# Adaptive layer norm, causal attention and a routed feed-forward layer on one core: maxima and masks fused, block masks spread over partitions by DMA

## The reference, cut to what matters

```python
mod = (silu(c) @ wmod)                      # six rows of 128: sa, ca, ga, sb, cb, gb
ga, gb = sign-preserving clamp of ga, gb to magnitude >= 0.25
h = layernorm(x) * (1 + ca) + sa            # x is (1, 2048, 128)
q, k, v = h @ Wq + bq, h @ Wk + bk, h @ Wv + bv
w = softmax(causal(q @ k.T / sqrt(128)))    # 2048 x 2048, causal
x = x + ga * ((w @ v) @ Wo + bo)
h = layernorm(x) * (1 + cb) + sb
prob = softmax(h @ w_router + b_router)     # 16 blocks; the 4 best are kept for each token
mask = top-4 of prob, one entry for each block of 32 hidden channels
y = relu(h @ w1.T + b1) * mask(per block) @ w2.T + b2     # 512 hidden channels
out = x + gb * y
```

## Time and profile before

| | |
|---|---|
| time, median of 3 runs | 129.37 us (129.15 to 129.53) |
| the profiled execution: its own time | 129.4 us |
| its span, first to last instruction | 127.7 us |
| mean granted clock of PE | 0.996 |
| PE busy | 120.7 us (95%) |
| DVE, ACT, POOL busy | 85.1, 75.5, 72.0 us |

### The profile page before, as it was taken

The page is one execution under the profiler, slowest core; times in us unless marked ns, Lnnn a source line. Parts: engine busy times, 40 slices in busy tenths (PEclk is TensorE's granted clock), DMA queues, the critical chain, the costliest instruction groups (busy, mean ns, idle before and its releaser), DMA issues.

```text
span 127.7 us, 2080 instructions
## 1 busy us (share of the span) xinstructions
PE 120.7 (95%) x655; PEld 95.2 (75%) x655; DVE 85.1 (67%) x300; ACT 75.5 (59%) x163; POOL 72.0 (56%) x112
## 2 busy tenths in 40 slices
PE   6999988999999999999999999979999999999980
PEld 2498747978798888889887878757987677767650
DVE  1688999997798798769692706971183557852650
ACT  2226487857384288976369949769721486173630
POOL 6068985962989149997857899939930330000000
PEclk9999999999999999999999999999999999999998
DMA  2993000000000000000000000000000002000205
GB/s 55 262 284 102 3 0 5 3 0 0 0 8 0 0 0 0 0 0 5 0 3 0 0 0 0 0 0 5 0 0 0 3 8 79 0 0 0 82 0 164
DMA packets 6656, 3.41 MB, mean 27 GB/s; under 512 B 1140, under 2 KB 6389, under 8 KB 6646
## 3 DMA queue, kind: packets, MB, share of 16 engines
q1 hardware_dynamic: 6214, 3.09, 8.6%
q10 hardware_dynamic: 432, 0.20, 0.5%
HBM read 2.24 MB, written 1.05 MB: 26 GB/s over the span
## 4 chain that ended last, share of the span: by engine, by line
PE 87%; DVE 9%; issue 1%; DVEq 0%
PE bank L719 19%; PE bank L723 18%; PE bank L720 18%; PE bank L767 7%; PE bank L935 4%; PE bank L939 3%; PE bank L820 3%; PE bank L850 3%; PE bank L743 2%; DVE g_hi L572 2%; PE bank L830 1%; DVE cmax L561 1%; PE bank L829 1%; PE bank L836 1%; PE bank L876 1%; DVE ldiff L601 1%
## 5 line engine op out<-in xcount | busy, mean ns | idle before, releaser
L376 POOL TENSOR_TENSOR p_lo<-p_full,p_hi 128x512 fp32r<-128x512 f32 (+3 forms) x40 | 44.1, 1123 | 16.3 <-ACT p_full L460 16.2
L453 ACT ACTIVATE p_hi<-bank 128x512 fp32r<-128x512 f32 (+3 forms) x40 | 21.5, 537 | 8.9 <-PE bank L798 4.9
L561 DVE TENSOR_REDUCE cmax<-bank 128x1 f32<-128x512 f32 (+3 forms) x36 | 21.9, 619 | 3.1 <-PE bank L767 1.8
L460 ACT ACTIVATE p_full<-bank 128x512 f32<-128x512 f32 (+3 forms) x40 | 21.4, 536 | 0.9 <-POOL p_lo L376 0.9
L621 DVE SCALAR_TENSOR_TENSOR hid_lo<-bank,hid_hi 128x512 fp32r<-128x512 f32 x16 | 10.9, 688 | 9.1 <-ACT hid_hi L480 9.1
L767 PE MATMUL bank<-zt_hi,g_hi 128*128 128x512 f32 (+3 forms) x40 | 15.5, 398 | 0.7 <-DVE cmax L561 0.3
L719 PE MATMUL bank<-g_hi,zt_hi 128*128 128x512 f32 (+3 forms) x40 | 15.6, 389 | 0.3 <-DVE g_hi L572 0.3
L719 PE MATMUL bank<-p_hi,z_hi 128*128 128x512 f32 (+3 forms) x40 | 15.5, 387 | 0.0
L723 PE MATMUL bank<-p_lo,z_hi 128*128 128x512 f32 (+3 forms) x40 | 14.7, 367 | 0.0
L720 PE MATMUL bank<-g_hi,zt_lo 128*128 128x512 f32 (+3 forms) x40 | 14.6, 364 | 0.0
L723 PE MATMUL bank<-g_lo,zt_hi 128*128 128x512 f32 (+3 forms) x40 | 14.5, 364 | 0.0
(11 more groups left out here) (164 smaller groups left out, 254.3 us busy)
## 6 DMA issues: line engine op xcount, KB each, us to landing
x<-in_L_attn_y_all_dram SPq DMA_DIRECT2D x4, 256.0 KB, 4.3
out_dram<-res SPq DMA_DIRECT2D x3, 256.0 KB, 2.3
w<-in_L_ffn_w_dram SPq DMA_DIRECT2D x2, 256.0 KB, 3.5
wmod<-in_L_wmod_dram SPq DMA_DIRECT2D x1, 256.0 KB, 5.1
out_dram<-res SPq DMA_DIRECT2D x2, 128.0 KB, 2.3
wmod<-in_L_wmod_dram ACTq DMA_DIRECT2D x1, 128.0 KB, 3.7
wk<-in_L_attn_Wk_dram SPq DMA_DIRECT2D x1, 64.0 KB, 3.3
wq<-in_L_attn_Wq_dram ACTq DMA_DIRECT2D x1, 64.0 KB, 3.5
```

The source lines that it names most:

```text
L376: pool.tensor_tensor(p_lo[:, s, w:], p_full[:, n % 2, w:], p_hi[:, s, w:].bitcast(F32), ALU.subtract).then_inc(p_lo_pool, 1)
L453: nc.scalar.activation(p_hi[:, s, w:], src, ACT.Exp).then_inc(p_hi_s, 1)
L460: nc.scalar.activation(p_full[:, n % 2, w:], src, ACT.Exp).then_inc(p_full_s, 1)
L561: nc.vector.tensor_reduce(cmax[:, n, c:c + 1], src, AX.X, ALU.max).then_inc(turn_out, 1)
```

## The change

It has these parts.

- **Row maxima.** The 16 additions of the triangle to the rough scores (line 769) go. DVE's reduction becomes a fused instruction that writes the chunk back into its bank and gives the running minimum of the negated values as an accumulator output; a chunk behind the first takes the result of the chunk before it as its bound. On a diagonal chunk the instruction also adds a table `future` (zeros and the triangle, from SBUF). The small second reductions (line 564) go. For groups 0 and 1 the maxima are transposed by four PE instructions (before: one), so that DVE adds them with one instruction of 1 by 512 (before: four of 1 by 128).
- **Head.** The turn is replaced by a simpler base (identity with a row of -1), so POOL's and DVE's sums over feature 0 go: four POOL instructions for a norm in place of six. Silu and the two gates and lift2 move from DVE to POOL (`z5`, `z6` there, a power in place of the reciprocal). POOL also makes `future` and `base`. 23 fillers `i` remain of 41.
- **Hidden layer.** In groups 0 to 2 the fourth PE instruction (line 850) goes, 12 of 16. The mask is now 1 or 0; SP spreads `route` by four DMAs a group within SBUF into `keep` (each reads 4 partitions of 1 KB and writes 128). DVE makes relu times mask from the PSUM bank into `hid_full` (two buffers), ACT rounds this to `hid_hi`, POOL subtracts to `hid_lo`. Group 3 stays as it was.
- **Last layer in two parts.** For group 3 the second projection runs as `d12` to `d15` over columns 0 to 255 and `d16` to `d19` over the others, in two banks; `y3` and `y4` follow.
- All four plans are new orders of these words.

```diff
 (the four plans are replaced by new orders)
-    last = mm(dst[:, 0:w], tile(g_hi, g * GT + r), zt_hi[:, c * GW:c * GW + w], start=True, stop=c < g)
-    if c == g:
-        last = mm(dst[:, w - P:w], ident_r[:], causal[:], start=False, stop=True)
+    mm(dst[:, 0:w], tile(g_hi, g * GT + r), zt_hi[:, c * GW:c * GW + w], start=True, stop=True).then_inc(turn_mm, 1)
...
+    so_far = FURTHEST if c == 0 else cmax[:, n, c - 1:c]
+    if c > 0:
+        dve.wait_ge(turn_out, turn_of[f"a{k - 1}"] + 1)
+    if c < g:
+        nc.vector.tensor_scalar(src, src, -1.0, so_far, ALU.mult, ALU.min,
+                                accum_out=cmax[:, n, c:c + 1]).then_inc(turn_out, 1)
+    else:
+        last = nc.vector.tensor_tensor_reduce(out=src, in0=src, in1=future[:, GW - w:], scale=-1.0,
+                                              scalar=so_far, op0=ALU.add, op1=ALU.min,
+                                              accum_out=nmax[:, g, Q * r:Q * r + 1])
...
+    if one_turn(g):                       # g >= 2
+        last = nc.tensor.transpose(tile(dst, 0), nmax[:, g, 0:P], ident[:])
+    else:
+        for r in range(GT):
+            last = nc.tensor.transpose(tile(dst, r), nmax[:, g, Q * r:Q * r + P], ident[:])
...
+    if spread(g):                         # g < 3, on SP, ahead of all the stores
+        sp.wait_ge(route_s, g + 1)
+        for m in range(NH):
+            sp.dma_start(keep[:, g, m, :],
+                         grp(route, g)[m * NBLK // NH:(m + 1) * NBLK // NH, :].rearrange(
+                             "e (o t) -> e o t", o=1).broadcast_to([NBLK // NH, BLK, GW])).then_inc(kept[g], 16)
...
+    if spread(g):                         # DVE, word h
+        dve.wait_ge(turn_mm, turn_of[f"h{n}"] + 1)
+        if m == 0:
+            dve.wait_ge(kept[g], 16 * NH)
+        if n >= 2:
+            dve.wait_ge(hid_lo_s, n - 1)
+        nc.vector.scalar_tensor_tensor(out=hid_full[:, n % 2, :], in0=turned_bank(f"h{n}")[:], scalar=0.0,
+                                       in1=keep[:, g, m, :], op0=ALU.max, op1=ALU.mult).then_inc(turn_out, 1)
+    # ACT, word h: nc.scalar.copy(hid_hi[:, m, :], hid_full[:, n % 2, :])
+    # POOL, word h: hid_lo = hid_full - hid_hi
...
+    three(y_bank(k)[:, part], tile(w2t_hi, m), tile(w2t_lo, m), hid_hi[:, m, part], hid_lo[:, m, part], ...)
```

More of the change, by code:

```diff
@@ L42 @@
[L42 to L45, removed]
+z0 i0 i1 i2 i3 i4 z1 i5 i6 i7 i8 i9 i10 i11 i12 z2 i13 i14 i15 n0 z3 i16 q0 i17 i18 i19 n1 a0 a1 i20 i21 i22
@@ new lines @@
+a2 a3 q1 n2 b0 a4 z4 a5 s0 a6 a7 s1 z5 a8 n3 a9 w0 a10 s2 q2 a11 s3 z6 a12 w1 b1 w2 a13 z8 z7 a14 s4 a15 s5
+a16 s6 a17 w3 a18 s7 a19 s8 a20 s9 a21 q3 a22 w4 a23 w5 a24 s10 b2 w6 a25 w7 a26 s11 a27 s12 s13 a28 a29 w8
+s14 a30 w9 s15 o0 s16 w10 w11 s17 a31 a32 s18 w12 w13 a33 s19 a34 w14 a35 z9 a36 s20 a37 w15 a38 s21 a39 w16
+s22 w17 b3 s23 w18 w19 s24 s25 n4 s26 w20 o1 s27 w21 w22 w23 r0 s28 o2 s29 s30 w24 m0 w25 s31 s32 h0 n5 w26
+w27 s33 w28 r1 s34 w29 w30 h1 h2 s35 s36 m1 w31 s37 n6 s38 w32 w33 r2 s39 w34 w35 w36 w37 w38 w39 h3 m2 d0 o3
@@ L145, in adaln_attention_sparse_ffn @@
         res = sb("res", [P, 2, GW])
+        future = sb("future", [P, GW])
         wq, wk, wv, wo = (sb(n, [P, P]) for n in ("wq", "wk", "wv", "wo"))
@@ L515, in norm_stats @@
                     last = nc.vector.bn_aggr(mv[:, k, g * GT + i, :], st[:, k, g * GT + i, :])
[L516 to L523, removed]
+                last.then_inc(stats, 1)
             def apply(n):
@@ L777, in turn_max @@
                 else:
-                    pe.wait_ge(nmax_s, GT * g)
-                nc.tensor.transpose(tile(dst, 0), nmax[:, g, :], ident[:]).then_inc(turn_mm, 1)
+                    pe.wait_ge(turn_out, turn_of[f"a{chunk_no(g, GT - 1, g)}"] + 1)
+                if one_turn(g):
+                    last = nc.tensor.transpose(tile(dst, 0), nmax[:, g, 0:P], ident[:])
+                else:
+                    for r in range(GT):
+                        last = nc.tensor.transpose(tile(dst, r), nmax[:, g, Q * r:Q * r + P], ident[:])
+                last.then_inc(turn_mm, 1)
             def score(t):
@@ L847, in hidden @@
                 if m == 0:
[L848 to L850 removed]
+                    pe.wait_ge(nt_lo_s, NG + g + 1)
+                    if not spread(g):
+                        pe.wait_ge(route_s, g + 1)
+                last = three(dst[:], tile(w1t_hi, m), tile(w1t_lo, m), grp(h_hi, g), grp(h_lo, g), stop=spread(g))
@@ L852, in down @@
+                if not spread(g):
+                    last = mm(dst[:], tile(pick, m), grp(route, g), start=False, stop=True)
+                last.then_inc(turn_mm, 1)
             def down(n):
-                g, m = n // NH, n % NH
+                k, m = n // NH, n % NH
+                g, part = group_part(k)
                 if m == 0:
-                    if g == 0:
+                    if k == 0:
                         pe.wait_ge(w2_lo_s, 1)
                         pe.wait_ge(q_lo_s, NG)
-                    elif g == 2:
+                    elif k == 2:
```

264 lines of the change are left out of this document (137 added, 127 removed).

## The result

| | before | after |
|---|---|---|
| time, median (lowest to highest) | 129.26 us (128.84 to 129.53, 4 runs) | 145.25 us (144.94 to 147.17, 4 runs) |
| ratio, 95% interval | | 1.124 [1.122, 1.127] |
| span of the profiled execution | 127.7 us | 145.4 us |
| PE, DVE, ACT, POOL busy | 120.7, 85.1, 75.5, 72.0 us | 121.5, 84.1, 76.4, 91.1 us |

The change makes the kernel 12% slower. The profiled execution of after is the one of 147.17 us, some 2 us above the others, so its spans are read with that in mind.

What follows compares the result with a forecast made beforehand. PE was taken as the bound, busy 120.7 of 127.7 us. Span: 127.7 - 2.8 - 0.6 - 0.15 + 0.2 - 0.45 + 0.8 + 0.4 = 125.1, plus 1.7 gives 126.8 us; range 124.4 to 128.7.

Steps and rivals of the forecast that it cites:

- the mask's way: Spreading the masks into keep by DMA: about 5 us in all, covered by 8.4 to 10.4 us of other work, costed at nothing.
- Masks late: Rival: mask DMAs on a quarter of the 16 engines take 7.4 us and DVE waits; 1.5 us, 128.3 us; chance 0.12.
- The fourth instruction: Hidden products: a PE instruction of 0.23 us goes 12 times, 2.8 us off PE, on the chain in full.
- z5: PE's step behind POOL's first gate: reached near 20.1, held until 22.2; net 0.2 us later than before.
- The head: Start of the kernel: silu's power 1.02 us on POOL; first projection at 11.3 in place of 11.83, 0.5 us gained.
- d4: Second projection on PE, after y0: a wait of 0.8 us for POOL's low half, bounds 0 and 2 us.
- The row maxima: Triangle additions off PE gain 1.0 us; fused maxima on DVE, 0.08 us dearer each, cost PE 0.4 (0 to 1.5).
- the rival in which DVE becomes the bound: Fused maxima 0.35 us dearer each exceed DVE's room between 12 and 60 us: 130.1 us; chance 0.12.
- ACT's copy of the masked relu: Hidden layer: ACT reads SBUF instead of the bank, 0.75 us each where the replaced row took 0.60.
- POOL's subtraction: Hidden layer: POOL makes the low halves in 12 subtractions of 1.29 us each.

Runs made afterwards that it cites:

- the version with the table: The changed kernel without the spreading DMAs, DVE multiplying by a 0/1 table in SBUF in place of the group's mask: 127.4 us, ratio 0.990 against the kernel before.

## Why the prediction was wrong

**The step that failed** is the mask's way: "I cost the DMAs at nothing, because other work covers them", with 5 us for ACT's copy, issue, latency and 512 KB at 284 GB/s. Measured, from the transposed mask of group 0 (74.2) to the last landing, are 18.5 us, and the cover ended after 8.6, when DVE stood ready; I had put it at 8.5 to 10.4. So the cover was right, and the cost of the transfers was 3.7 times too small. The rate was taken from the loads from HBM in the head, with 16 engines and 17.8 GB/s for each. These transfers used about 3.5 engines, and each moved 7 GB/s for the first 8 us. The issues, which I had put at a part of 1 us, took 8.7 us. Both factors of the rate count: with 14 engines at 6.5 GB/s the same 512 KB took 5.6 us and were in time, and with 4 engines at 17.8 GB/s they would have taken 7.4 by my own arithmetic, with issue and latency still more than the cover.

**The rival that was right.** "Masks late" named the place, the shape of the transfers and the quarter of the engines, and got 0.12 and a price of 1.5 us. The Trainium skill (DMA: Bandwidth & Descriptors, Why a DMA increments its semaphore by 16 and not by 1) gives four engines for these DMAs; the trace agrees, a share of 0.20 to 0.24 of 16 engines is 3.2 to 3.8. Two things were missing in its price. The rate of an engine was still that of the loads; at the 24 GB/s measured first the move alone would have come out at 22 us (it took 16.5, because the rate rose later), and either is more than the cover of group 0 and that of group 1, 14.3 us. And a wait of 9.4 us costs more than itself, since the steps behind it run at the 1.2 GHz level until the clock is granted again.

**The whole loss in numbers.** In the profile the span is 145.4 against 125.7 us in the version with the table, whose orders are the same: 19.7, of which 14.3 are waits for `hid_full` and 5.4 the rest. The two timelines, laid side by side, say what the rest is. Until the first transposed mask of group 0 after is 1.5 us behind (73.8 against 72.3), by the lower clock after `z5` in this execution, which the other version's profile doesn't have. Behind the first wait the same words (h2, s35, s36, m1 and the start of w31) take 5.2 us in place of 2.9, and behind the second (h6, y0, h7 and d4) 4.6 in place of 3.0. That is 1.5 + 2.3 + 1.6 = 5.4: slow steps at a clock of 0.50, which leave nothing for the orders.

**The rest of the forecast**, read against the version with the masks there (127.4 us; span 125.7 where I forecast 125.1):
- The fourth instruction, 2.8 us: it went 12 times, with 0.23 us of PE each. Without it the order of DVE can be another, and in these orders it is worth 5.2. So the term held by itself, and I had missed what hangs on it.
- `z5`: PE waited there 1.94 us as forecast, until 22.61 in place of 22.2, so 0.6 later than before and not 0.2.

```profile
22.61 0.46 PE L962 MATMUL bank<-wo,wv_t 128*128 128x128 f32 x2 [1.94 <-POOL ga_wide L384]
```

- The head: silu's power took 0.58 us, not 1.02, and the first projection started at 10.67 in place of my 11.3.
- `d4`: no wait there, 0.8 us too dear.
- `m3`: PE waits 1.1 us for the masks of the last group; I had not seen it. 125.1 + 0.4 - 0.8 + 1.1 = 125.8 us of span against 125.7. That this comes out so near is in part luck: several terms were off in opposite directions, and no run prices the head or the two-part last layer alone.
- The row maxima: DVE's groups by form in after (busy us, mean ns, idle before):

```profile
L626 DVE TENSOR_SCALAR_CACHE_REDUCE bank<-bank,cmax 128x512 f32<-128x512 f32 x12 | 9.1, 757 | 1.4 <-PE bank L811 0.4
L626 DVE TENSOR_SCALAR_CACHE_REDUCE bank<-bank 128x512 f32<-128x512 f32 x12 | 8.4, 699 | 3.4 <-PE bank L811 3.4
...
L629 DVE CUSTOM_DVE_ANT_0 bank<-bank,future,cmax 128x512 f32<-128x512 f32 x3 | 2.3, 759 | 1.2 <-PE bank L811 0.9
...
L629 DVE DVE_READ_ACCUMULATOR2_ANT nmax<- 128x1 f32 x16 | 2.3, 141 | 0.0
...
L626 DVE DVE_READ_ACCUMULATOR bank<-bank 128x1 f32 x12 | 1.7, 141 | 0.0
```

Each maximum has the companion that the Trainium skill (VectorE: DVE Perf Modes, Two Vector instructions with no wait between them) describes, and it takes 0.141 us, near my upper bound of 0.16 and not the 0.08 that I took; the main instruction is 0.70 to 0.76 us in place of 0.69. With that, the price of one is 0.84 to 0.90 us and not 0.77. It didn't matter: the rival in which DVE becomes the bound did not come about, since DVE was busy for 37.7 of the 48 us from 12 to 60 in after, and for 39.1 in the version with the masks there at a clock of 1.00, where it had been 41.4.
- ACT's copy of the masked relu took 0.62 us (forecast 0.75) and POOL's subtraction 1.28 (1.29).

What stays open: why the four engines moved 24 GB/s first and twice as much later, and why the third and fourth issue held SP for so long.

## What to carry to other kernels

Price a transfer by its number of engines, by the rate of one engine in a transfer of the same kind, and by the time that its issues take; the peak of the loads says nothing of a small spread within SBUF. Where a spread reads few partitions, look for an order of the data in which it reads 16: here dealing the channels in turn to the tiles took 17.6 us off, and made one transfer do for four. And when an order of work is written out for a form in which one engine no longer waits for another, undoing that form can cost more than its instructions: here 5.2 us for 2.8 of instructions, as long as the orders stay. The best version found here, one wide DMA a group and the gate a step later, takes 126.91 us, 1.7% less than the kernel before.

## What the runs showed of the hardware that I had not expected

Spreads within SBUF moved 6.5 to 7 GB/s for each busy engine in the first microseconds, a bit over a third of the 17.8 of the loads. In after the rate of the same four engines then doubled, in group 0 just when POOL, the last of the compute engines, had stopped (same columns as above):

```profile
84.00:85.00 1.00, 0.05 (x1) 0.00 (x0) 0.00 (x0) 0.00 (x0) 0.56 (x1) 1.00 0.21 22
85.00:86.00 1.00, 0.00 (x0) 0.00 (x0) 0.00 (x0) 0.00 (x0) 0.00 (x0) 1.00 0.25 45
86.00:87.00 1.00, 0.00 (x0) 0.00 (x0) 0.00 (x0) 0.00 (x0) 0.00 (x0) 1.00 0.24 60
```

That looks as if the engines' work on SBUF slowed the transfers, but that isn't what sets the rate. In group 1 of the same trace it rose while PE and DVE worked:

```profile
110.00:113.00 3.00, 3.00 (x14) 2.23 (x12) 2.01 (x12) 0.78 (x1) 1.18 (x4) 1.00 0.24 51
```

In the version in which nobody waits for the DMAs it rose from 26 to 63 GB/s although PE, DVE and POOL were as busy as before, and ACT only somewhat less:

```profile
77.00:85.00 8.00, 8.00 (x42) 6.69 (x41) 4.02 (x20) 6.95 (x16) 6.80 (x9) 1.00 0.22 26
86.00:95.00 9.00, 9.00 (x59) 7.93 (x57) 4.69 (x21) 5.33 (x13) 7.83 (x8) 1.00 0.25 63
```

In all three places the rise comes 1 to 2 us after SP has got out the fourth DMA of the group (83.5 and 107.6 us in after, 83.8 in the other version). Whether the issuing slows the moving, no run here separated. PE's granted clock fell to 0.50 in both waits, and the steps behind them went at 0.43 in place of 0.23 us. And the third of four such DMA issues held SP's queue for 3.8 us in both groups of the chain, the fourth for 3.5 to 3.6, so a transfer behind them on that queue would have been late as well.
